# One core, a routed feed-forward block twice around attention: the third norm reordered, the identity built by VectorE, and x's first load split

## The reference

```
x = x + 0.5 * ffn(layernorm(x))      # 8 experts, the same weights both times
x = x + attention(layernorm(x))      # 16 heads of 16, causal, S = 4096
x = x + 0.5 * ffn(layernorm(x))

ffn: logits = x @ gate_w + gate_b;  probs = softmax over the tokens
     each token picks its 2 best experts, weighted by probs
     y[e] = relu(relu(relu(x@w1[e]+b1)@w2[e]+b2)@w3[e]+b3)
     v[e] = sum over the tokens of y[e] * weight;  out = sum of v[e] over the token's two experts
```

## Time and profile before

| what | value |
|---|---|
| runs | 2202.78, 2195.99 and 2198.48 us, median 2198.48 |
| profiled execution, its time | 2204.46 us |
| its span | 2202.7 us |
| first norm, from the span's start to `route(0)`'s first step | 0 to 34.47 us |
| third norm, from the first transposed head to `route(1)`'s first step | 1871.8 to 1930.18 us |
| mean granted TensorE clock | 0.975 of full speed |

### The profile page before, as it was taken

One profiled execution on the slowest core, in us unless ns is written; L12 is line 12 of the kernel. 1 busy time (PEld: TensorE's weight loads), 2 busy tenths in 40 slices (PEclk: granted clock), 3 DMA queues, 4 the chain that ended last, 5 costly groups with the idle time before them and its releaser, 6 DMA issues.

```text
span 2202.7 us, 97616 instructions
## 1 busy us (share of the span) xinstructions
PE 2120.6 (96%) x42439; PEld 1851.5 (84%) x42443; DVE 1848.5 (84%) x3894; ACT 1624.4 (74%) x3567; POOL 515.3 (23%) x1295
## 2 busy tenths in 40 slices
PE   5999989999999999999999999999999999969998
PEld 3788865599999999999999999998999997748885
DVE  7666666999999999999999999999999995666665
ACT  5344456688888888888888888888888888334442
POOL 1333213413122131221212213122121211023330
PEclk8899999999999999999999999999999999969998
DMA  8211114301010010100101001010010100331112
GB/s 276 64 45 48 35 38 141 96 19 33 4 32 22 16 33 4 32 23 13 33 4 33 23 13 32 4 33 24 12 33 4 32 4 6 113 106 46 49 48 84
DMA packets 94853, 94.32 MB, mean 43 GB/s; under 512 B 41108, under 2 KB 83864, under 8 KB 94424
## 3 DMA queue, kind: packets, MB, share of 16 engines
q0 software_dynamic: 41376, 42.91, 7.6%
q1 hardware_dynamic: 52704, 45.15, 6.4%
q10 hardware_dynamic: 344, 0.01, 0.0%
HBM read 62.24 MB, written 25.43 MB: 40 GB/s over the span
## 4 chain that ended last, share of the span: by engine, by line
PE 91%; DVE 5%; ACT 1%; issue 1%; DMA 1%; another core or an unknown queue 0%; POOL 0%; DVEq 0%; ACTq 0%; SPq 0%
PE bank L1233 44%; PE bank L1225 19%; PE bank L1109 17%; PE bank L1175 2%; PE bank L1271 2%; PE bank L1187 1%; PE bank L1120 1%; PE bank L1336 1%; DVE stats L1366 1%; PE bank L1127 1%; PE bank L1279 1%; PE bank L994 1%; DVE x_res L1686 0%; DVE rows L1388 0%; DVE work L1555 0%
## 5 line engine op out<-in xcount | busy, mean ns | idle before, releaser
L1233 PE MATMUL bank<-work 96*32 96x512 bf16 (+4 forms) x17920 | 1415.8, 363 | 2.9 <-DVE work L1725 2.5
L926 ACT ACTIVATE feat<-bank 128x512 f32<-128x512 f32 (+3 forms) x2304 | 1250.9, 565 | 156.4 <-PE bank L1233 78.7
L1725 DVE TENSOR_REDUCE work<-bank 128x1 f32<-128x512 f32 (+3 forms) x2176 | 1299.7, 639 | 64.7 <-PE bank L1233 53.0
L1225 PE MATMUL bank<-feat,phase 128*17 128x128 f32 x16896 | 1140.2, 272 | 2.3 <-issue 2.3
L1225 PEld LDWEIGHTS bank<-feat,phase 128*17 128x17 f32 x16896 | 831.6, 98 | 67.2 <-issue 2.9
L1233 PEld LDWEIGHTS bank<-work 96*32 96x32 bf16 (+1 forms) x17920 | 810.2, 96 | 69.1 <-DVE work L1725 10.8
L1109 PE MATMUL bank<-work 128*128 128x256 f32 (+1 forms) x1872 | 398.3, 363 | 0.5
L1109 PEld LDWEIGHTS bank<-work 128*128 128x128 f32 x1872 | 325.5, 192 | 36.6 <-DVE work L1617 0.8
L601 POOL TENSOR_SCALAR_AFFINE_SELECT feat<-feat 128x128 f32<-128x128 f32 x512 | 146.3, 293 | 447.4 <-ACT feat L926 442.7
L543 POOL DMA_INDIRECT work<-token_table,row_no x142 | 138.0, 972 | 302.7 <-PE bank L1120 149.5
L1617 DVE COPY work<-phase 128x514 f32 x234 | 101.2, 435 | 121.9 <-ACT work L840 97.0
(11 more groups left out here) (195 smaller groups left out, 1392.8 us busy)
## 6 DMA issues: line engine op xcount, KB each, us to landing
phase<-in_w SPq DMA_DIRECT2D x12, 1024.0 KB, 12.2
work<-qk_parts POOLq DMA_DIRECT2D x60, 192.0 KB, 3.7
token_table<-rows SPq DMA_DIRECT2D x8, 1056.0 KB, 8.7
qk_parts<-phase SPq DMA_DIRECT2D x20, 384.0 KB, 2.8
work<-qk_parts POOLq DMA_DIRECT2D x60, 128.0 KB, 4.2
qk_parts<-work SPq DMA_DIRECT2D x12, 384.0 KB, 2.6
x_res<-in_x SPq DMA_DIRECT2D x8, 512.0 KB, 7.6
work<-work SPq DMA_DIRECT2D x256, 1.0 KB
```

The source lines that it names most:

```text
L926: eng.activation(p_ring[:, n % P_RING, lo:QB], s_bank("probs", n)[:, lo:QB], ACT.Exp, scale=HD ** -0.5).then_inc(sig.s_done, 1)
L1225: mm = eng.matmul(bank[ACC_BANK][GRID * g:GRID * g + VW, 0:P], v_aug[:, t, h, :], p_ring[:, n % P_RING, g * P:(g + 1) * P], start=(t == 0) ...
L1233: mm = eng.matmul(out[GRID * g:GRID * (g + 1), width], left[:, GRID * g:GRID * (g + 1)], right, start=start, stop=stop)
L1725: eng.tensor_reduce(maxima[:, h % 2, j, i, k + 1:k + 2], scores[:, 0:hi - lo], AX_X, ALU.max).then_inc(sig.a_done, 1)
```

## The change

Four things are changed.

1. `ident` is made by DVE instead of POOL: a memset of ones, a scan that makes the numbers 0 to 127 along the row, a transposition in blocks of 32x32 that puts each partition's number within its block of 32 into a column, and four comparisons, one for 32 partitions each. `rows` serves as the scratch. The semaphore `gate_pad` becomes `begun` and also counts these seven instructions; PE waits for `begun`, not for `ident_at`. POOL's memset and affine select for `ident` go, its other constants stay in their order.
2. x is loaded in eight loads as before, of 2, 2, 4, 4, 4, 4, 4 and 8 tiles.
3. PE and ACT get an order of their own for the third norm. DVE's stays, and so do the groups of eight tiles of its statistics.
4. `copy_feat` and `transpose_rows` take four tiles at a call; for the first and second norm that is the order as before.

The core of the diff:

```diff
+X_LOADS = (0, 2, *range(4, NT - 4, 4), NT)
+BLOCK = 32
+BEGUN = 5 + P // BLOCK
...
-            triangle(ident[:, :], 0.0, ALU.not_equal, 1.0)
-            ident_at[0] = n_const[0]
...
-            for g in range(NT // LN_GRP[0]):
-                a, b = g * LN_GRP[0], (g + 1) * LN_GRP[0]
-                eng.dma_start(x_res[:, a:b, :], x_rows[:, a:b, :]).then_inc(sig.x_loaded[g], 16)
+            for n, (a, b) in enumerate(zip(X_LOADS, X_LOADS[1:])):
+                eng.dma_start(x_res[:, a:b, :], x_rows[:, a:b, :]).then_inc(sig.x_loaded[n], 16)
...
+            def third_norm():                                 # ACT
+                copy_heads(0)
+                copy_heads(1)
+                copy_heads(2)
+                for g in range(GROUPS):
+                    if 2 * g + 3 < NT // 4:
+                        copy_heads(2 * g + 3)
+                    sqrt_of(2, g)
+                    if 2 * g + 4 < NT // 4:
+                        copy_heads(2 * g + 4)
+                    copy_feat(2, 2 * g)
+                    if g:
+                        copy_gate(1, 2 * g - 2)
+                        copy_gate(1, 2 * g - 1)
+                    copy_feat(2, 2 * g + 1)
+                copy_gate(1, GATES - 2)
+                copy_gate(1, GATES - 1)
...
-                need.wait_ge(sig.const, ident_at[0])
+                need.wait_ge(sig.begun, BEGUN)
...
+            def third_norm():                                 # PE
+                attended(0)
+                for g in range(GROUPS):
+                    if g + 1 < GROUPS:
+                        attended(g + 1)
+                    transpose_rows(2, 2 * g)
+                    if g:
+                        gate(1, 2 * g - 2)
+                        gate(1, 2 * g - 1)
+                    transpose_rows(2, 2 * g + 1)
+                    if g:
+                        gate_rows(1, 2 * g - 2)
+                        gate_rows(1, 2 * g - 1)
+                gate(1, GATES - 2)
...
+            def identity():                                   # DVE, between its two memsets and the first norm
+                numbers, row = rows[:, 0, 0:P], rows[:, 1, 0:BLOCK]
+                eng.memset(rows[:, 2, 0:P], 1.0).then_inc(sig.begun, 1)
+                need.wait_ge(sig.begun, 3)
+                eng.tensor_tensor_scan(numbers, rows[:, 2, 0:P], rows[:, 2, 0:P], -1.0, ALU.mult,
+                                       ALU.add).then_inc(sig.begun, 1)
+                need.wait_ge(sig.begun, 4)
+                eng.transpose(row, numbers[:, 0:BLOCK]).then_inc(sig.begun, 1)
+                need.wait_ge(sig.begun, 5)
+                for r in range(0, P, BLOCK):
+                    eng.tensor_scalar(ident[r:r + BLOCK, :], numbers[r:r + BLOCK, :], rows[r:r + BLOCK, 1, 0:1], float(r),
+                                      ALU.subtract, ALU.is_equal).then_inc(sig.begun, 1)
+                need.wait_ge(sig.begun, BEGUN)
```

More of the change, by code:

```diff
@@ L254, in __init__ @@
         self.const = one("constants")
-        self.x_loaded = many("x_loaded", NT // LN_GRP[0])
-        self.gate_pad, self.small = one("gate_padded"), one("small_loads")
+        self.x_loaded = many("x_loaded", len(X_LOADS) - 1)
+        self.begun, self.small = one("begun"), one("small_loads")
         self.attw = one("attention_weights")
@@ L729, in copy_feat @@
                     need.wait_ge(sig.out_mm, b * KD)
[L730 to L735, removed]
+                for k in range(KD):
+                    need.wait_ge(sig.tr[n], 4 * (g * KD + k + 1))
+                    eng.activation(feat[:, k, a * P:b * P], bank[k][:, :], ACT.Copy).then_inc(sig.feat[n], 1)
             def copy_gate(f, m):
@@ L965, in _ @@
             attention()
-            layer_norm(2, attended, nothing)
+            third_norm()
             route(1)
@@ L975, in transpose_rows @@
             def transpose_rows(n, g):
-                need.wait_ge(sig.const, ident_at[0])
[L977 to L995, removed]
+                need.wait_ge(sig.begun, BEGUN)
+                i0 = 4 * g
+                for k in range(KD):
+                    need.wait_ge(sig.feat[n], g * KD + k - 1)
+                    if n == 1:
+                        need.wait_ge(sig.xt_copy[0], N_TILES)
+                        need.wait_ge(sig.w_row[0], N_TILES)
+                    if n == 2:
+                        need.wait_ge(sig.s_done, S_ALL)
+                    for i in range(i0, i0 + 4):
+                        by_vector = LN_GRP[0] - BY_SCALAR
+                        if n:
+                            need.wait_ge(sig.normed[n], i + 1)
+                        elif i - i0 < by_vector:
+                            need.wait_ge(sig.normed[0], g * by_vector + i - i0 + 1)
+                        else:
+                            need.wait_ge(sig.normed_s, g * BY_SCALAR + i - i0 - by_vector + 1)
+                        eng.transpose(bank[k][:, (i - i0) * P:(i - i0 + 1) * P], rows[:, i, k * P:(k + 1) * P],
+                                      ident[:, :]).then_inc(sig.tr[n], 1)
             def gate(f, m):
@@ L1029, in first_norm @@
                 gate_rows(0, GATES - 1)
[L1031 to L1037, removed]
+            def third_norm():
[5 more added lines that the diff above has]
+                    if g:
                         gate(1, 2 * g - 2)
                         gate(1, 2 * g - 1)
-                    transpose_rows(n, g)
-                    if n == 2 and g:
+                    transpose_rows(2, 2 * g + 1)
+                    if g:
                         gate_rows(1, 2 * g - 2)
                         gate_rows(1, 2 * g - 1)
[L1044 to L1052, removed]
+                gate(1, GATES - 2)
+                gate(1, GATES - 1)
+                gate_rows(1, GATES - 2)
+                gate_rows(1, GATES - 1)
             def chosen_rows(f, m0, m1):
@@ L1360, in statistics @@
                     if n == 0:
-                        need.wait_ge(sig.x_loaded[g], 16)
+                        need.wait_ge(sig.x_loaded[sum(b <= i for b in X_LOADS[1:])], 16)
                     elif n == 1:
```

36 lines of the change are left out of this document (7 added, 29 removed).

## The result

The changed kernel takes 2204.68 us (median of ten runs, 2199.99 to 2210.03), the kernel before 2198.01 (ten runs, 2195.03 to 2203.92). The ratio is 1.0029, with a 95% interval of 1.0019 to 1.0040: 6.4 us slower, between 4.2 and 8.8. The forecast was +1.0 us, with 2194.5 to 2204.5 us as the range of the median; the measured median lies 0.2 us above that range. On two other occasions, on the chips that the record numbers 13 and 14, the same kernel gave 1.0011 (1.0002 to 1.0020) and 1.0008 (0.9997 to 1.0020), that is about +2.4 and +1.8 us.

The account below looks back on a forecast made before the run. DVE was taken to bound the first norm, DVE and PE in turn the third. Terms -0.35 + 0 + 0.6 + 0.75 = +1.0 us on the median 2198.48 gave 2199.5 us, range 2194.5 to 2204.5.

Parts of the forecast that it names:

- What bounds the stages: First and third norm: DVE sets the pace in the first; DVE and PE hold each other in turn in the third.
- Identity by VectorE, term 0: First norm: seven added DVE instructions end at about 2.8 us, hidden by the wait for x; 0 us.
- First load in two, term -0.35: First norm: DVE starts at about 4.2 us, tiles 4 to 7 land no earlier, later groups move up; -0.35 us.
- Up to the sixth projection, term 0: Third norm up to O5: O3 still waits for DVE's addition, C5 fits ACT's gap, O5 ends as before; 0 us.
- Third group, term +0.6: Third norm: root 2 behind C7 delays DVE by 0.85 us, of which 0.24 is free; +0.6 us.
- The end, term +0.75: Third norm's end: G4 and G5 move onto the path behind R6, +1.08 us; R7's saved wait, -0.31 us.
- the second rival: Third norm's end: a 1.7 us PE pause ahead of R6 halves the clock; +2.95 us, 2201.4 us; chance 22%.
- The sum: Whole kernel: load, third-group and end terms together make it +1.0 us slower, counted as no change.
- The order pays: First and third norm: C7 ends before root 2 is due, loads land early; -0.15 us, 2198.3 us; chance 13%.
- The identity is late: First norm: DVE's identity delays the statistics; +0.95 us in place of -0.35, 2200.8 us; chance 3%.
- Slower than before: Restart of the experts after the second routing: slow clock reaches it; +8.5 us, 2207.0 us; chance 4%.

Follow-up runs that it names:

- pairs_first: Kernel before with the new third-norm order, root 2 and gates G4, G5 moved back, plus DVE adding the next group's first two banks before normalising; ratio 0.9984.
- third_only: Kernel before with the new PE and ACT order of the third norm as only edit; ratio 1.0010 (0.9998 to 1.0021).
- after: The changed kernel's first profiled execution, set against the kernel before; this execution took 2199.99 us.
- after_again: The changed kernel unaltered, run again beside the kernel before; ratio 1.0011 (1.0002 to 1.0020).
- after_other: The changed kernel unaltered, run a third time beside the kernel before; ratio 1.0008 (0.9997 to 1.0020).
- third_root: Kernel before with the new third-norm order, but root 2 again ahead of the last four tiles' head copies; 2193.0 us in a single run.

## Why the prediction was right or wrong

**That "no change" held is in part luck.** The forecast said +1.0 us and took anything under 6.6 us for no change; the first comparison gave 6.4, inside that bound by 0.2 us, and the median lies 0.2 us outside the range. One term of the sum had the wrong sign and another left the clock out.

**What bounds the stages: right.** DVE in the first norm, DVE and PE in turn in the third. pairs_first shows it from the other side: only a change of DVE's order shortened the stage.

**Identity by VectorE, term 0: right.** Done at 3.09 us against a forecast of 2.8. The scan took 0.42 and not 0.35, the memset 0.17, the transposition 0.21, the comparisons about 0.3 each and not 0.2. The cover ended at 4.05, so 1 us of it was left.

**First load in two, term -0.35: wrong, in sign.** The first half did land as worked out (DVE at 4.05, forecast 4.2), and the second half kept VectorE waiting for only about 0.1 us. The step that failed is "The bytes in front are the same, so it will not land earlier", taken as if it couldn't land later. It took for granted that a load lands a fixed time after its bytes are due. With two short loads 16 to 37% of the rate is missing in the window from 5 to 6 us (293 to 218 GB/s against 345 to 348), which by the bytes moved is 0.3 us at most, and this load lands 1.3 to 2.1 us after its bytes are due, not 0.7. Tiles 4 to 7 are begun at 7.83, 8.15, 7.16 and 7.85 us in four profiles, against 6.73 to 6.95 (median 6.78) with loads of four tiles. The routing's first step comes at 35.5, 36.1, 34.7 and 35.4 us, on average 35.4, against 34.3 to 34.6 in the nine profiles with loads of four tiles in front: +1.0 us, not -0.35. No bound of the prediction reached beyond 0 for this term. Why it lands so late is open.

**Up to the sixth projection, term 0: right at equal clock.** O3's start hangs on VectorE whatever ACT does: it comes 18.3 us behind T0 in third_only as in before. The one pause of 2.87 us in after is the former two joined. The loss to the slow clock up to O3 is 0 to 1.7 us in the six profiles of the old order (mean 1.1) and 0 to 3.0 in the seven of the new one, mended or not, with VectorE's order unchanged (mean 1.6). Whether the longer pause makes it larger is not shown by so few.

**Third group, term +0.6: right in mechanism, measured 0.49.** Root 2 came right behind C7. The delay was 0.49 us (0.77 - 0.28) and not 0.85, for T7 came 6.83 us behind O5's start in place of 7.41 (third_only against before), 0.58 earlier and not 0.31, and C7 with it. Nothing of the delay was free: from this group's normalising to the next one's it is 11.85 us in both kernels. The 0.24 us that the prediction took off was a wait ahead of the second addition, and behind it VectorE waits another 1.22 us for O7 in before, so nothing hangs on it.

**The end, term +0.75: right for the moved gates, but the clock came on top.** The gates moved onto the path as said, and the pause they left drew the clock down. That was the second rival, given 22%: it is what happens. In all five profiles with the new tail (after, after_again, after_other, third_only, third_root) the pause ahead of R6 is about 2.0 us and R6 takes 2.2; in eight with G4 and G5 ahead of R6 it is at most 0.86 and R6 takes 1.73 or 1.74. The ninth, pairs_first, has a pause of 1.42 us and lost the clock too, which speaks for the pause and against the gates' place as the cause. The tail takes 7.9 to 8.3 us in place of 6.24, that is 1.7 to 2.1 more: 0.9 to 1.3 are what R6 and the gates behind it took beyond 1.74 and 1.08 us, and the 0.7 left are the moved gates. The rival had put 1.95 on the clock. The sentence that failed is "Against it: the end before had several short pauses and kept the full clock": the short pauses were no guide for one of 2 us, and the earlier trace rows had shown what such a pause can do. The rule of the Trainium skill, "TensorE: Matmul & The Clock Gate", section "HAM oscillation — how this bites in real kernels", that the work behind an idle stretch starts at half rate, agrees with the trace here, where the granted clock is 0.52 behind 2.03 us of idle time. Ahead of O3 it agrees less well: of 13 profiles with a pause of 1.9 to 2.9 us there, 7 had the slow clock behind it.

**The sum.** By the stages +1.0 (loads) + 0.5 (root) + 1.8 (tail, median of five) = +3.3 us, against +1.0 forecast. The three comparisons give +6.4, +2.4 and +1.8, on average 3.5. The intervals of the second and third (0.4 to 4.4 and -0.7 to 4.4) hold the 3.3; that of the first, which starts at 4.2, does not. Some 3 us of the first result have no cause here. What the profiles offer is that the experts' stages, with the same instructions, took 217.1 and 219.0 us in the profile before and 215.2 and 216.7 in that after, but 211.8 to 213.4 in all twelve profiles of the experiments. The second norm and attention took 1582.4 to 1588.3 us over all profiles, also with the same instructions. There is room there for such a difference. It wasn't shown to be the cause.

**Other rivals.** "The order pays" fell with the root's place. "The identity is late" fell. "Slower than before" named the restart of the experts; `route(1)` and the stage behind it took no longer than before, so its mechanism didn't occur, though the kernel was slower: from 1959 to 1970 us, where the second experts begin in after, the granted clock was 0.89 on average and not 0.5.

## What to carry to other kernels

Work that stands in a pause of the matmul engine can be worth more than its own length, for here it kept the clock up: before moving it out, add its length to the pause that stays, and look in several traces for what a pause of that length did elsewhere. A single one can mislead, as O3 shows. In a list that is run in its written order, a short operation that a busy engine waits for (here a square root of 0.2 us) goes ahead of long copies, even if these feed the engine that seems to be the bound. Where two engines hold each other in turn, look for the releasing instruction (an addition that frees a bank) queued behind work that nobody waits for yet, and move that.

## What the runs showed of the hardware that was not expected

Two DMAs of 256 KB ahead of those of 512 KB brought the first bytes to use 0.8 to 1.0 us earlier. Tiles 4 to 7, the third load, were taken up 0.4 to 1.4 us later than with four-tile loads, with 218 GB/s in place of 347 in one window, though queue, bytes and order of tiles were the same.

Ahead of R6, whose matmuls are paced by VectorE, a pause of 1.4 to 2.0 us was followed by a granted clock of 0.5 in six profiles of six, and one of up to 0.86 us in none of eight. Ahead of O3 a pause of 1.9 to 2.9 us was followed by it in 7 of 13, and executions of one and the same kernel differed (after_again lost it there, after_other did not).

A block transposition of 128x32 f32 on VectorE took 0.21 us, a scan of 128 f32 0.42 us, and a comparison of 32x128 f32 with a per-partition operand 0.28 us, two thirds of the 0.41 us that the normalising of 128x256 took.
